# Expert layer of a two-layer gated attention kernel: first layer feature-major, weight fetched per slot

## The reference

```python
logits = xf @ Wr + br
topk_val, topk_idx = jax.lax.top_k(logits, K)               # K = 2 of E = 8
scores = jax.nn.softmax(topk_val, axis=-1)
h = jnp.einsum('nd,edh->enh', xf, W1) + b1[:, None, :]      # 256 -> 1024
a, g = jnp.split(h, 2, axis=-1)
act = jax.nn.silu(a) * g                                    # 512
out_e = jnp.einsum('enh,ehd->end', act, W2) + b2[:, None, :]
```

## Time and profile before

| | |
|---|---|
| median of 3 runs | 1054.1 us (1053.96 to 1055.47) |
| the profiled execution, its own time | 1055.81 us |
| its span (first to last instruction) | 1053.8 us |
| mean granted TensorE clock | 0.954 of 2.4 GHz |
| TensorE busy | 967.2 us (92%) |
| VectorE, ScalarE, GpSimd busy | 546.5, 435.3, 423.9 us |
| DMA over the whole span | 47.71 MB, mean 45 GB/s |

### The profile page before, as it was taken

How to read it: one execution, slowest core, us unless ns; L and a number is a source line. 1 busy time by engine, 2 the same in 40 slices (tenths; PEclk the granted TensorE clock), 3 DMA queues, 4 the chain that set the end, 5 groups by cost and what they waited for, 6 DMA issues and landing times.

```text
span 1053.8 us, 18112 instructions
## 1 busy us (share of the span) xinstructions
PE 967.2 (92%) x5884; PEld 784.0 (74%) x5885; DVE 546.5 (52%) x1186; ACT 435.3 (41%) x1316; POOL 423.9 (40%) x537
## 2 busy tenths in 40 slices
PE   5999999999998829999999998789999999989995
PEld 3599999999997715555555555589999999986663
DVE  7555455454544552222232225677777776663363
ACT  0254545555453202222222223355565555535442
POOL 5253433333342013343433434575666544332242
PEclk9899999999999659999999999899999999999987
DMA  9600000000000563111111113200000000000002
GB/s 286 267 1 1 1 0 1 1 2 2 0 1 1 219 231 95 40 40 40 40 50 40 40 40 121 53 21 21 14 17 20 11 11 1 1 2 0 1 1 80
DMA packets 29015, 47.71 MB, mean 45 GB/s; under 512 B 4493, under 2 KB 23105, under 8 KB 28705
## 3 DMA queue, kind: packets, MB, share of 16 engines
q1 hardware_dynamic: 25553, 37.68, 10.7%
q0 software_dynamic: 3408, 9.31, 3.4%
HBM read 37.68 MB, written 9.31 MB: 45 GB/s over the span
## 4 chain that ended last, share of the span: by engine, by line
PE 83%; DVE 8%; DMA 3%; issue 2%; POOL 2%; ACT 2%; POOLq 0%; DVEq 0%; SPq 0%; ACTq 0%
PE banks L1480 11%; PE banks L477 9%; PE banks L479 9%; PE banks L478 8%; PE banks L511 8%; PE banks L485 6%; PE banks L1519 6%; PE banks L496 6%; PE banks L503 3%; PE banks L626 3%; DMA region_b<-xn_rows,token_now 2%; PE banks L1693 2%; PE banks L1505 1%; PE banks L343 1%; PE banks L412 1%
## 5 line engine op out<-in xcount | busy, mean ns | idle before, releaser
L1480 PE MATMUL banks<-W,region_b 128*128 x312 | 150.1, 604 | 0.6 <-ACT region_b L1527 0.6
L1235 POOL TENSOR_TENSOR region_a<-region_a,recip 128x512 f32<-128x512 f32 x64 | 66.6, 1041 | 177.9 <-DVE recip L847 177.9
L1084 ACT ACTIVATE region_a<-banks,negmax 128x154 f32<-128x154 f32 x256 | 96.2, 389 | 91.0 <-DVE negmax L841 88.5
L1270 POOL TENSOR_TENSOR region_a<-region_a,recip 128x640 f32<-128x640 f32 x64 | 80.3, 1255 | 107.6 <-DVE recip L953 107.3
L1566 DVE TENSOR_TENSOR region_b<-banks,region_a 128x512 f32<-128x512 f32 x78 | 53.9, 692 | 115.5 <-PE banks L1480 115.5
L1614 POOL TENSOR_TENSOR region_b<-region_b 128x512 f32<-128x512 f32 x39 | 49.4, 1266 | 148.3 <-DVE region_b L1566 148.3
L511 PE MATMUL banks<-region_a 128*128 128x128 f32 x768 | 96.6, 275 | 1.6 <-DVE oT_low L864 1.5
L511 PEld LDWEIGHTS banks<-region_a 128*128 128x128 f32 x768 | 91.0, 192 | 2.4 <-issue 1.7
L1480 PEld LDWEIGHTS banks<-W,region_b 128*128 128x128 f32 x312 | 55.7, 193 | 44.7 <-issue 43.6
L1543 ACT COPY region_b<-banks 128x512 f32<-128x512 f32 x39 | 22.9, 586 | 152.9 <-PE banks L1505 152.9
L1519 PE MATMUL banks<-region_a,region_b 128*128 x312 | 76.1, 387 | 7.4 <-issue 6.6
(11 more groups left out here) (241 smaller groups left out, 2379.6 us busy)
## 6 DMA issues: line engine op xcount, KB each, us to landing
W<-in_L_ffn_W SPq DMA_DIRECT2D x1, 8192.0 KB, 27.2
y_slots<-region_b SPq DMA_DIRECT2D x39, 128.0 KB, 1.7
region_a<-in_L_ffn_b SPq DMA_DIRECT2D x1, 4096.0 KB, 19.5
region_a<-in_L_ffn_W SPq DMA_DIRECT2D x1, 4096.0 KB, 30.5
region_b<-in_L_xattn_Wq SPq DMA_DIRECT2D x2, 1024.0 KB
xn_rows<-region_b SPq DMA_DIRECT2D x1, 2048.0 KB, 8.6
out<-x SPq DMA_DIRECT2D x4, 512.0 KB, 3.0
region_b<-in_L_xattn_Wk SPq DMA_DIRECT2D x2, 768.0 KB
```

Source lines behind the costliest of these rows:

```text
L1084: e = act.activation(pr[:, j, 0:L.keys], scores[:, g % 2, u, i * L.keys:(i + 1) * L.keys], ACT.Exp, bias=negmax[:, g % 2, j:j + 1], accum_ ...
L1235: pool.tensor_tensor(whole, pr[:, :, 0:split], rc.broadcast_to([P, L.hs, split]), ALU.mult)
L1270: pool.tensor_tensor(probs1[:, n % 2], probs1[:, n % 2], rc, ALU.mult).then_inc(sem("p_norm"), 1)
L1480: mm = pe.matmul(banks[:, 2 * r + part, :], xgT[:, r, k, :], w, start=(k == 0), stop=(k == DK - 1))
```

## The change

- First layer feature-major: a 128x128 piece of W1 is stationary and x (128 columns) moves, 16 matmuls per slot instead of 4. The result has hidden features on partitions, so the biases become one column each (`b1`, made by one transpose and one copy at the start of routing), ScalarE's SiLU reads PSUM with the bias inside, four pieces per slot, and VectorE does (g + bias) * silu(a) in four fused pieces. The product is already in the form that the second layer takes: no transposes of it, no copy, no multiply on GpSimd.
- TensorE's body of slot j is now: whole first layer of j+1, x's transposes for j+2, second layer of j.
- W1 is no longer resident: SyncE loads the expert's 1 MB for each slot into one of three buffers in region_a, as soon as the slot that used the buffer has had its first layer. W2 (4 MB) takes the place of half of W1 in the W region and is loaded at the start of the kernel.
- Three buffers instead of two for gathered rows, x transposed, products and outputs; the loop runs over three slots; gathers run three slots ahead.

```diff
@@ -70,7 +70,8 @@
-    assert SLOTS % 2 == 1
+    RING = 3
+    assert SLOTS % RING == 0
@@ -126,8 +127,9 @@
-        w1_region = sb("W1", [P, E * DK * H2])
-        W1 = w1_region[:].rearrange("p (e k n) -> p e k n", e=E, k=DK)
+        W2_SIZE = E * HK * D
+        w1_region = sb("W1", [P, W1_SIZE])
+        W2 = w1_region[:, 0:W2_SIZE].rearrange("p (e k n) -> p e k n", e=E, k=HK)
@@ -162,8 +164,11 @@
-        b1 = reg_a.part(E * H2, "p (e n) -> p e n", e=E)
-        W2 = reg_a.part(E * HK * D, "p (e k n) -> p e k n", e=E, k=HK)
+        W1 = reg_a.part(RING * DK * H2, "p (r k n) -> p r k n", r=RING, k=DK)
+        reg_a.part(2 * RING * H)
+        a_act = reg_a.part(RING * H, "p (r m n) -> p r m n", r=RING, m=HK)
+        act_sum = reg_a.part(RING * H, "p (r m n) -> p r m n", r=RING, m=HK)
+        reg_a.at = 2 * W2_SIZE
@@ -185,13 +190,11 @@
-        xg = reg_b.part(2 * D, "p (r d) -> p r d", r=2)
-        xgT = reg_b.part(2 * D, "p (r k n) -> p r k n", r=2, k=DK)
-        y_slot = reg_b.part(2 * D, "p (r d) -> p r d", r=2)
-        a_act = reg_b.part(2 * H, "p (r n) -> p r n", r=2)
-        g_act = reg_b.part(2 * H, "p (r n) -> p r n", r=2)
+        xg = reg_b.part(RING * D, "p (r d) -> p r d", r=RING)
+        xgT = reg_b.part(RING * D, "p (r k n) -> p r k n", r=RING, k=DK)
+        y_slot = reg_b.part(RING * D, "p (r d) -> p r d", r=RING)
+        reg_b.at = 6 * INNER + NC * D - 2 * H
...
-        actT = reg_b.part(2 * H, "p (r k n) -> p r k n", r=2, k=HK)
@@ -1303,6 +1309,8 @@
+            pe.wait_ge(sem("b1_in"), 16)
+            pe.transpose(misc_ps[:, 0:E * 2 * HK], b1_rows, ident[0:E * 2 * HK, 0:E * 2 * HK]).then_inc(sem("b1_ps"), 1)
@@ -1422,6 +1430,8 @@
         def act_routing(act):
+            act.wait_ge(sem("b1_ps"), 1)
+            act.copy(b1, misc_ps[:, 0:E * 2 * HK].rearrange("p (e m) -> p e m", e=E)).then_inc(sem("b1_ready"), 1)
@@ -1432,151 +1442,157 @@
+        ROUNDS = SLOTS // RING
         def slot_bodies(eng, emit):
...
-            with eng.Fori(1, SLOTS // 2 - 1) as i:
+            with eng.Fori(1, ROUNDS - 2) as i:
...
-            emit(SLOTS // 2 - 1)
-            emit(SLOTS // 2)
+            emit(ROUNDS - 2)
+            emit(ROUNDS - 1)
...
         def is_tile(j):
...
         def body_tiles(i):
-            return [(2 * i + r, r) for r in range(2) if is_tile(2 * i + r)]
+            return [(RING * i + r, r) for r in range(RING)]
...
         def owner_of(eng, j):
...
+        def after(r, n):
+            return (r + n) % RING, (r + n) // RING
         def sp_experts(sp):
...
-            sp.wait_ge(sem("xn_stored"), 16)
+            w1 = t_in["L0_ffn_W1"].rearrange("e (k p) n -> p e k n", p=P)
+            def load_w1(j, r):
+                e = owner_of(sp, j)
+                sp.dma_start(W1[:, r], w1[:, bass.ds(e, 1)].rearrange("p a k n -> p (a k) n")).then_inc(sem(f"w1_in{r}"), 16)
+            sp.wait_ge(sem("owner_ready"), 1)
+            for j in range(RING):
+                load_w1(j, j)
+            sp.wait_ge(sem("hg_ps"), 1)
+            load_w1(RING, 0)
...
             def emit(i):
...
+                    if is_tile(j + 4):
+                        sp.wait_ge(sem("hg_ps"), j + 2)
+                        load_w1(j + 4, after(r, 1)[0])
...
-                    if first and r == 0:
+                    if isinstance(j, int) and j == 0:
+                        sp.wait_ge(sem("xn_stored"), 16)
...
         def pe_experts(pe):
-            pe.wait_ge(sem("w1_in"), 16)
...
-            def turn_x(j, i, r):
+            def turn_x(r, i):
...
-            def hidden(e, r, part):
-                for k in range(DK):
-                    w = W1[:, bass.ds(e, 1), k, part * H:(part + 1) * H].rearrange("p a n -> p (a n)")
-                    mm = pe.matmul(banks[:, 2 * r + part, :], xgT[:, r, k, :], w, start=(k == 0), stop=(k == DK - 1))
-                mm.then_inc(sem("hg_ps" if part else "ha_ps"), 1)
-            turn_x(0, 0, 0)
-            e = owner_of(pe, 0)
+            def hidden(r, i):
+                pe.wait_ge(sem(f"w1_in{r}"), 16 * (i + 1))
+                for part in range(2):
+                    for m in range(HK):
+                        cols = slice(part * H + m * P, part * H + (m + 1) * P)
+                        for k in range(DK):
+                            mm = pe.matmul(banks[:, 2 * r + part, m * P:(m + 1) * P], W1[:, r, k, cols], xgT[:, r, k, :],
+                                           start=(k == 0), stop=(k == DK - 1))
+                    mm.then_inc(sem("hg_ps" if part else "ha_ps"), 1)
+            turn_x(0, 0)
...
-            hidden(e, 0, 0)
-            turn_x(1, 0, 1)
-            hidden(e, 0, 1)
+            hidden(0, 0)
+            turn_x(1, 0)
...
             def emit(i):
...
-                    final = not is_tile(j + 1)
-                    if not final:
-                        e_next = owner_of(pe, j + 1)
+                    if is_tile(j + 1):
...
-                        if not (first and r == 0):
-                            pe.wait_ge(sem("a_read"), j)
-                        hidden(e_next, 1 - r, 0)
+                        hidden(after(r, 1)[0], i + after(r, 1)[1])
+                    if is_tile(j + 2):
+                        turn_x(after(r, 2)[0], i + after(r, 2)[1])
+                    e = owner_of(pe, j)
...
-                    if not first:
-                        pe.wait_ge(sem("at_sb"), j - 1)
-                    for k in range(HK):
-                        mm = pe.transpose(banks[:, 4 + r, k * P:(k + 1) * P], a_act[:, r, k * P:(k + 1) * P], ident[:])
-                    mm.then_inc(sem("at_ps"), 1)
-                    if not final:
-                        if not (first and r == 0):
-                            pe.wait_ge(sem("g_read"), j)
-                        hidden(e_next, 1 - r, 1)
-                    if is_tile(j + 2):
-                        turn_x(j + 2, i + 1, r)
-                    e = owner_of(pe, j)
-                    pe.wait_ge(sem("at_sb"), j + 1)
-                    if not (first and r == 0):
+                    if not (isinstance(j, int) and j == 0):
...
-                        mm = pe.matmul(o_ps[:, 0:D], actT[:, r, k, :], w, start=(k == 0), stop=(k == HK - 1))
+                        mm = pe.matmul(o_ps[:, 0:D], act_sum[:, r, k, :], w, start=(k == 0), stop=(k == HK - 1))
...
         def act_experts(act):
+            act.wait_ge(sem("owner_ready"), 1)
             def evacuate_x(j, r):
...
             def silu(j, r):
-                act.wait_ge(sem("a_read"), j + 1)
-                act.activation(a_act[:, r, :], a_act[:, r, :], ACT.Silu).then_inc(sem("silu_done"), 1)
+                e = owner_of(act, j)
+                act.wait_ge(sem("ha_ps"), j + 1)
+                for m in range(HK):
+                    last = act.activation(a_act[:, r, m, :], banks[:, 2 * r, m * P:(m + 1) * P], ACT.Silu,
+                                          bias=b1[:, bass.ds(e, 1), m:m + 1].rearrange("p a n -> p (a n)"))
+                last.then_inc(sem("silu_done"), 1)
...
+            silu(0, 0)
...
-            silu(0, 0)
...
             def emit(i):
...
-                    act.wait_ge(sem("at_ps"), j + 1)
-                    if not first:
-                        act.wait_ge(sem("ey_ps"), j - 1)
-                    act.copy(actT[:, r], banks[:, 4 + r, :].rearrange("p (k n) -> p k n", k=HK)).then_inc(sem("at_sb"), 1)
...
-                        silu(j + 1, 1 - r)
+                        silu(j + 1, after(r, 1)[0])
...
-                        evacuate_x(j + 2, r)
+                        evacuate_x(j + 2, after(r, 2)[0])
...
         def dve_experts(dve):
...
-            dve.wait_ge(sem("b12_in"), 32)
-            def inputs(j, r, wait_free):
+            dve.wait_ge(sem("b1_ready"), 1)
+            dve.wait_ge(sem("b2_in"), 16)
+            def gated(j, r, reused):
...
-                for part, buf, ps, read in ((0, a_act, "ha_ps", "a_read"), (1, g_act, "hg_ps", "g_read")):
-                    dve.wait_ge(sem(ps), j + 1)
-                    if wait_free:
-                        if part == 0:
-                            dve.wait_ge(sem("at_ps"), j - 1)
-                        else:
-                            dve.wait_ge(sem("act_ready"), j - 1)
-                    dve.tensor_tensor(buf[:, r, :], banks[:, 2 * r + part, :],
-                                      b1[:, bass.ds(e, 1), part * H:(part + 1) * H].rearrange("p a n -> p (a n)"),
-                                      ALU.add).then_inc(sem(read), 1)
-            inputs(0, 0, False)
+                dve.wait_ge(sem("silu_done"), j + 1)
+                dve.wait_ge(sem("hg_ps"), j + 1)
+                if reused:
+                    dve.wait_ge(sem("ey_ps"), j - 2)
+                for m in range(HK):
+                    last = dve.scalar_tensor_tensor(act_sum[:, r, m, :], banks[:, 2 * r + 1, m * P:(m + 1) * P],
```

(63 more changed lines are left out.)

2 lines of the change are left out of this document (removed).

## The result

The changed kernel takes 1024.7 us in the median (1023.4 to 1025.3), the kernel before 1054.8 beside it: a ratio of 0.971, 95% interval 0.970 to 0.973. It is 30 us faster; I forecast 10, and the range ended 3 us too high. Two further sets of runs gave 1023.0 and 1023.5.

A forecast was written before the change was run, and what follows sets the result against it. It took TensorE's own stream plus a few pauses in the expert stage as the bound. Slots -7.8, start -1.2, end -0.8: -9.8 us from 1055.8 to 1046.0, the median 1.7 lower at 1044.3 us; range 1028 to 1053.

The forecast's parts named there:

- Register loads: Before each second layer: less queued work covers the expert-number load, so a 0.43 us pause in every slot.
- Gather waits: TensorE's expert-stage pauses for gathered rows, 7.0 us in all, should go with gathers three slots ahead.
- First layer, narrow: Expert first layer on TensorE: 32 instructions of 0.112 us make 3.58 us instead of 3.43, +0.15 per slot.
- The rival's price: First layer's narrow matmuls paced by their weight loads: +2.4 us per slot over the forecast, 1130 us; chance 0.02.
- Transposes of the product: Ahead of the second layer: the feature-major product needs none, -0.43 us per slot on TensorE.
- Start: Up to slot 0's second layer: it begins at 402.8 instead of 403.97, -1.2 us.
- End: Slots 36 to 38: 8.66 us instead of 9.50, -0.8 us.
- ScalarE and VectorE at nothing: Expert stage: four SiLUs (1.1 to 1.6 us) and four fused operations (1.2 to 1.9) stay covered, costing nothing.
- DMA: Expert-stage weight stream: 3.4 to 4.0 us per MB, queues 0.7 to 0.8 full, covered.
- The rival of late gathers: Gathers late behind weights: pauses of 0.2 to 0.3 us per slot stay, within 2 us of 1054; chance 0.07.
- The rival with the load hidden: Register load hidden before the second layer: interval 5.53 to 5.65, 1024 to 1029 us; chance 0.22, in part or whole.

The follow-up runs named there:

- e1: The kernel before, with the gather and the copy of the next token numbers issued ahead of GpSimd's multiply; 1037.0 us, ratio 0.983.
- e8: e1 with the first layer cut into 128-column matmuls, still token-major; 1040.4 us.
- e9: e1 without the product's transposes and ScalarE's copy of them, so the output isn't the reference's; 1016.4 us, ratio 0.965.
- e13: The changed kernel with each weight asked for one slot later, as two buffers would force it; 1029.7 us, ratio 0.977.
- e7: The changed kernel with each slot's weight fetched twice, the second time into unused space; 1055.0 us.

## Why the prediction was wrong, point by point

- **Register loads: the step that failed.** It said: "Bounds: 0 if the sequencer can run further ahead on short instructions", and took 0.43 us "since the load's start beside the wide matmul shows how many instructions it passes". It doesn't. In that slot the gather was issued at 525.59 and took 3.0 us to land, so the rows were there at 528.6, and the load began at 528.8: it marks the end of a wait, not the end of a queue. The slot with the pause reads the same way: gather issued at 519.7, 3.2 us to land, load at 522.9. I had read even the cheap slots as full queues, when they were gathers that landed just in time. In e1, with the rows there early, the load starts 3.0 us ahead of the second layer. Measured in the changed kernel: 1.9 us ahead, and no pause. 0.43 + 0.10 (the second layer behind a pause) + 0.02 in 36 slots is 20 us, as much as the error of the forecast (1044.3 against 1024.7).
- **Gather waits.** "7.0 us in all, should go" was misread: 4.5 of them are the first gather, which no slot can hide, and it is 4.6 now. Only 2.5 us lay in the slots. But late gathers cost 17 to 18 us by e1, since the pauses put down to "issue" and the extra matmul gaps behind them had the same cause. The sum hid this, because it took the interval whole.
- **First layer, narrow.** Right: +0.15 forecast, +0.14 in e8. The rule of the Trainium skill ("TensorE: Matmul & The Clock Gate", "Back-to-back issue gap"), by which it would have been a factor of 2.5, didn't hold for this fp32 shape: 0.112 four times against 0.429, a factor of 1.04. The rival's price was worked out a little wrong: 6.2 less 3.58 is +2.6 us a slot, not +2.4.
- **Transposes of the product.** Right: -0.43 forecast, -0.44 in e9. The three steps together (pauses, narrow matmuls, transposes), -0.48, +0.14 and -0.44, make -0.78, the difference between 6.296 and 5.518.
- **Start.** -1.2 forecast, -1.5 in the trace, but the absolute times show nothing. The changed kernel began the second layer of slot 0 at 402.44 in one trace and at 399.90 in another, and there the whole stage is 2.5 us earlier from its first transposes on, for a reason that lies ahead of it. From the first matmul of the first layer to the second layer of slot 0 it is 10.3 us in both, against 12.2 before and 10.8 in e1 (389.30 to 400.07). So the start gained 1.9 us, and 1.4 of them are late rows and what they held up.
- **End.** -0.8 forecast, -1.5 measured: slot 36 to 37 has no pause either (5.30), and slot 38 waits for VectorE's add as forecast (2.73 against 2.60).
- **ScalarE and VectorE at nothing.** Right. Four SiLUs took 1.14 us and four fused operations 1.13, at or just under the low ends, and no second layer but the last waits for VectorE.
- **DMA.** The share was forecast at 0.7 to 0.8 and is 0.71. The price of a MB was too high by a quarter to a half. The rival of late gathers was right in its cause (4.9 instead of 3.0 us) and wrong in its effect, since the gathers are issued three slots ahead.
- **The cases.** The rival with the load hidden gave 1024 to 1029, and this is what happened. I gave it 0.22 and cut the range in its middle. A bound that I had no row against belonged in the range whole.

## What to carry to other kernels

Here TensorE's register load waited behind transposes whose rows had not landed, so a late transfer cost its lateness (0.20 us per slot) plus the load behind it (0.28). Before reading a limit off the moment at which a sequencer starts something, look at what landed just then. A gather issued ahead of a multiply instead of behind it gave 18 us; the whole restructuring, which contains that step, gave 30.

A stream added to the queues must be weighed by what it does to the small transfers beside it. How early these are issued is part of the change: with its gathers issued two slots later the same kernel is slower than the one before. How many buffers that takes has to be counted from the waits; here two would probably have done for the gathers, and for the weights the third one gave 6 us.

## What the runs showed of the hardware that I had not expected

- The TensorE sequencer ran 1.7 us ahead of x's transposes in the changed kernel, some 15 fp32 matmul instructions of 0.112 us, and 2.8 us ahead of them in e1 (load at 490.2, transposes at 492.97), where nothing held it at the gathered rows.
- One wait of 3.3 us on TensorE (e13) was followed by matmuls at a mean granted clock of 0.58, and cost 6.4 us instead of 3.3. In e7 a wait of 2.2 us was followed by 5 us at 0.71. The waits of the kernel before, 0.6 us at most between 404 and 630, did no such harm: the stage kept a clock of 1.00.
- Loads of 4 KB rows reached 379 GB/s at a share of 1.01 in e7, where the key and value weights beside little else ran at 241 and 0.91 in the kernel before.
- A gather of 128 rows of 1 KB went from 2.8 us without the stream to 4.9 with it, though the queues were only 0.71 full.
